# Held sums between two recurrent layers, and normalisation block by block ahead of the first sweep

## What is computed

```
x = x + L0(gn(x))    # attention over channels with a depthwise 3x3 convolution
x = x + L1(gn(x))    # four sweeps: down, up, right, left
x = x + L2(gn(x))    # the same with other weights
x = x + L3(gn(x))    # a gated MLP over tokens
gn(v): 16 groups of 3 channels; (v - mean) / sqrt(var + 1e-5) over channels and pixels
sweep: carry = row[i] + conv1d(carry, w, 5 taps) + b ; out[i] = carry
```

## Time and profile before

| what | value |
|---|---|
| median of 3 runs | 2726.66 us (2725.55 to 2729.71) |
| the profiled execution, time | 2723.77 us |
| its span, first to last instruction | 2721.6 us |
| mean granted TensorE clock | 0.95 |
| TensorE busy | 2385.1 us, 88% |
| VectorE busy | 1333.7 us, 49% |
| ScalarE busy | 770.9 us, 28% |
| GpSimd busy | 212.5 us, 8% |

### The profile page before, as it was taken

The page is one execution under the profiler, slowest core; times in us unless marked ns, Lnnn a source line. Parts: engine busy times, 40 slices in busy tenths (PEclk is TensorE's granted clock), DMA queues, the critical chain, the costliest instruction groups (busy, mean ns, idle before and its releaser), DMA issues.

```text
span 2721.6 us, 45615 instructions
## 1 busy us (share of the span) xinstructions
PE 2385.1 (88%) x18588; PEld 2127.3 (78%) x18588; DVE 1333.7 (49%) x3212; ACT 770.9 (28%) x1190; POOL 212.5 (8%) x259
## 2 busy tenths in 40 slices
PE   1999999999999799999999990599999999952785
PEld 1999948957953399999999990599999999951453
DVE  3323354344355544444555557444444555566855
ACT  3533254354356400243002551200441000002441
POOL 2000000000000180000000004500000000000311
PEclk9999999999999899999999995799999999976888
DMA  8840000004001320000000008500000000049734
GB/s 154 146 86 7 1 1 1 1 1 93 1 1 24 70 48 1 1 1 1 1 1 1 1 1 252 131 1 1 1 1 1 1 1 1 1 126 268 243 104 128
DMA packets 75558, 129.88 MB, mean 48 GB/s; under 512 B 10224, under 2 KB 59600, under 8 KB 70448
## 3 DMA queue, kind: packets, MB, share of 16 engines
q1 hardware_dynamic: 68064, 123.36, 19.0%
q10 hardware_dynamic: 7184, 3.84, 0.6%
q0 software_dynamic: 128, 0.01, 0.0%
HBM read 76.85 MB, written 50.33 MB: 47 GB/s over the span
## 4 chain that ended last, share of the span: by engine, by line
PE 80%; DVE 6%; DMA 5%; ACT 4%; issue 2%; SPq 2%; POOL 1%; ACTq 0%; POOLq 0%; DVEq 0%
PE bank L978 18%; PE bank L979 16%; PE bank L980 16%; PE bank L881 14%; PE bank L943 6%; PE bank L896 3%; PE bank L886 3%; ACT work L644 3%; DMA work<-saved 2%; PE bank L1087 2%; DMA work<-in_x 1%; DMA saved<-image 1%; SPq L335 1%; PE bank L1058 1%; DMA image<-flat_rows 1%
## 5 line engine op out<-in xcount | busy, mean ns | idle before, releaser
L1302 DVE TENSOR_TENSOR image<-bank,image 112x128 f32<-112x128 f32 x2032 | 660.4, 325 | 712.8 <-PE bank L980 712.8
L978 PE MATMUL bank<-image,scan_wt 112*112 112x128 f32 x4064 | 808.3, 280 | 36.4 <-ACT image L718 29.7
L979 PE MATMUL bank<-image,scan_wt 112*112 112x126 f32 x4064 | 770.9, 271 | 0.0
L980 PE MATMUL bank<-image,scan_wt 112*112 112x126 f32 x4064 | 769.7, 270 | 0.0
L978 PEld LDWEIGHTS bank<-image,scan_wt 112*112 112x112 f32 x4064 | 566.1, 175 | 40.6 <-ACT image L718 29.9
L979 PEld LDWEIGHTS bank<-image,scan_wt 112*112 112x112 f32 x4064 | 581.2, 176 | 0.0
L980 PEld LDWEIGHTS bank<-image,scan_wt 112*112 112x112 f32 x4064 | 578.6, 176 | 0.0
L881 PE MATMUL bank<-work 112*128 112x192 f32 x2304 | 423.9, 332 | 10.5 <-issue 10.5
L644 ACT ACTIVATE work<-image,gn_shift,gn_scale 48x567 f32<-48x567 f32 (+5 forms) x384 | 334.6, 904 | 317.0 <-PE bank L886 220.3
L881 PEld LDWEIGHTS bank<-work 112*128 112x128 f32 x2304 | 374.9, 192 | 12.9 <-issue 12.4
L736 ACT COPY work<-image 48x256 f32 x192 | 80.3, 418 | 731.7 <-PE bank L980 731.3
(11 more groups left out here) (151 smaller groups left out, 1496.6 us busy)
## 6 DMA issues: line engine op xcount, KB each, us to landing
work<-saved SPq DMA_DIRECT2D x64, 384.0 KB, 10.4
image<-flat_rows SPq DMA_DIRECT2D x4, 3072.0 KB, 18.7
out<-image SPq DMA_DIRECT2D x8, 1536.0 KB, 7.2
saved<-image SPq DMA_DIRECT2D x12, 768.0 KB, 9.9
saved<-image SPq DMA_DIRECT2D x6, 1536.0 KB, 15.6
flat_rows<-image SPq DMA_DIRECT2D x46, 192.0 KB, 6.1
band<-in_x SPq DMA_DIRECT2D x16, 384.0 KB, 5.4
work<-in_x SPq DMA_DIRECT2D x16, 384.0 KB, 5.4
```

Of the source, the lines that this page charges most:

```text
L978: mm(dst, wt[:, 1], src, start=True, stop=False)
L979: mm(dst[:, 1:J2, :], wt[:, 0], src[:, 0:J2 - 1, :], start=False, stop=False)
L980: mm(dst[:, 0:J2 - 1, :], wt[:, 2], src[:, 1:J2, :], start=False, stop=True).then_inc(s_prod[g], 1)
L1302: v.tensor_tensor(line(g, along_w, at), prod, line(g, along_w, src), ALU.add).then_inc(s_state[g], 1)
```

## The change

- The unit between the layers becomes the piece (two runs of 1024 elements of a pair) in place of the chunk. VectorE adds the even pieces, GpSimd the odd ones.
- `back` has six buffers (`GAP`): the five `kept` and one more. Six pieces are fetched ahead. While piece t < `HELD` = 10, its sum is written in place and piece t + 6 is fetched into its buffer. The sums of the last six pieces are written into their buffers, `summed(t)`, and `image` keeps layer 1's raw result there until the normalisation reads the held sum and writes `image`.
- Every piece is saved by itself as soon as it is summed; the last six are saved from the buffers.
- The normalisation of both layers is split: block 0 of pair 0 on ScalarE and block 0 of pair 1 (piece 8) on VectorE let the first sweep start. In layer 1, ScalarE then does blocks 1 to 7 of both pairs; in layer 2 it does all of pair 0 first and blocks 1 to 7 of pair 1 after the norm of pair 1. `s_ready` counts them, and TensorE and VectorE wait for it at every sixteenth row of the first sweep. `s_tail` is gone.
- The four normalisations between the stages of the last output convolution are gone.
- Before an in-place normalisation an engine waits only for the save of what it overwrites: the quarter in layer 1, the pieces of the pair below 10 in layer 2, nothing for held sums.
- GpSimd's constants and SyncE's fetches for the token stage now wait for `s_late` (the last six saves) and `s_ready`.

```diff
-VCH = 2
-V_COLS = 5120
+GAP = 6
+HELD = 2 * (K2 // 8) - GAP
-        back = kept[0:PER]
+        back = kept + [cut(at - 256 - CHUNK, [CHUNK], P)]
...
+        def piece(buf, t):
+
+            if buf is image:
+                g, n = t // NBLK, t % NBLK
+                v = image[0:P, g * 2 * IMG:(g + 1) * 2 * IMG].rearrange("p (s n) -> p s n", s=2)
+                return v[:, :, n * 2 * BN:(n + 1) * 2 * BN]
+            return buf.rearrange("p (s n) -> p s n", s=2)
+
+        def summed(t):
+
+            return piece(image if t < HELD else back[t % GAP], t).rearrange("p s (n b) -> p b s n", b=2)
+
+        def unsaved(eng, layer, t):
+
+            if layer == 0:
+                eng.wait_ge(*((s_save, 32) if t < NBLK else (s_raw[t % NBLK // 2], 32)))
+            elif t < HELD:
+                eng.wait_ge(s_keep[t // NBLK], 32 * (NBLK, HELD - NBLK)[t // NBLK])
...
-            for c in range(PER):
-                bring(c)
-            for b in range(NB - 1):
-                for m in range(PER):
-                    if m < VCH:
-                        sp.wait_ge(s_kept_v, b * VCH + m + 1)
-                    else:
-                        sp.wait_ge(s_kept_p, b * (PER - VCH) + m - VCH + 1)
-                    bring((b + 1) * PER + m)
-                save_columns(b, 0, IMG)
-            sp.wait_ge(s_kept_v, NB * VCH)
-            save_columns(NB - 1, 0, VCH * CHUNK)
-            sp.wait_ge(s_kept_p, NB * (PER - VCH))
-            save_columns(NB - 1, VCH * CHUNK, IMG)
-            sp.wait_ge(s_keep[0], 64)
-            sp.wait_ge(s_keep[1], 96)
+            for t in range(GAP):
+                bring(t)
+            for t in range(2 * NBLK):
+                sp.wait_ge((s_kept_v, s_kept_p)[t % 2], t // 2 + 1)
+                if t < HELD:
+                    bring(t + GAP)
+                save(t, s_keep[t // NBLK] if t < HELD else s_late)
+            sp.wait_ge(s_keep[0], 32 * NBLK)
+            sp.wait_ge(s_keep[1], 32 * (HELD - NBLK))
+            sp.wait_ge(s_late, 32 * GAP)
+            sp.wait_ge(s_ready, 2 * (NBLK - 1))
...
-            for m in range(KEPT):
-                nc.gpsimd.memset(kept[m][32:HALF, :], 0.0).then_inc(s_back_gap, 1)
+            for m in range(GAP):
+                nc.gpsimd.memset(back[m][32:HALF, :], 0.0).then_inc(s_back_gap, 1)
...
+            for t in range(1, 2 * NBLK, 2):
+                pool.wait_ge(s_back[t % GAP], 32 * (t // GAP + 1))
+                dst = piece(image if t < HELD else back[t % GAP], t)
+                nc.gpsimd.tensor_tensor(dst, piece(image, t), piece(back[t % GAP], t), ALU.add).then_inc(s_kept_p, 1)
+
+            pool.wait_ge(s_late, 32 * GAP)
+            pool.wait_ge(s_ready, 2 * (NBLK - 1))
...
+            def normalise(layer, t):
+
+                act.wait_ge(s_gn, 2 * layer + 3 + t // NBLK)
+                unsaved(act, layer, t)
+                src = summed(t) if layer else piece(image, t).rearrange("p s (n b) -> p b s n", b=2)
+                dst = piece(image, t).rearrange("p s (n b) -> p b s n", b=2)
+                for i in range(2):
+                    b = t // NBLK * 2 + i
+                    last = nc.scalar.activation(dst[:, i], src[:, i], ACT.Identity, bias=gn_shift[0:P, b:b + 1],
+                                                scale=gn_scale[0:P, b:b + 1])
+                return last
...
-                elif 2 <= n < 6:
-                    last = normalise(0, n // 2 - 1, n % 2 * SUB, (n % 2 + 1) * SUB)
-            last.then_inc(s_state[0], 1)
...
-                    for b in range(2):
-                        last = normalise(layer, b, 0, IMG)
-                    last.then_inc(s_state[0], 1)
+                normalise(layer, 0).then_inc(s_state[0], 1)
+                for n in range(1, NBLK if layer else 1):
+                    normalise(layer, n)
                 deviation(2 * layer + 3, 2, NB)
-                for b in (2, 3):
-                    last = normalise(layer, b, V_COLS, IMG)
-                last.then_inc(s_tail, 1)
+                for n in range(1, NBLK):
+                    if layer == 0:
+                        normalise(layer, n)
+                    normalise(layer, NBLK + n).then_inc(s_ready, 1)
...
+                if scan == 0 and at and at % 16 == 0:
+                    pe.wait_ge(s_ready, layer * (NBLK - 1) + at // 16)
...
-                pe.wait_ge(s_tail, layer + 1)
...
+                if scan == 0 and at % 16 == 0:
+                    dve.wait_ge(s_ready, layer * (NBLK - 1) + at // 16)
...
+                    for t in range(0, 2 * NBLK, 2):
+                        dve.wait_ge(s_back[t % GAP], 32 * (t // GAP + 1))
+                        dst = piece(image if t < HELD else back[t % GAP], t)
+                        v.tensor_tensor(dst, piece(image, t), piece(back[t % GAP], t), ALU.add).then_inc(s_kept_v, 1)
+                        if t % NBLK:
+                            sums(t - 1)
+                        last = sums(t)
+                        if t % NBLK == NBLK - 2:
+                            sums(t + 1).then_inc(s_stat, 2)
+                        if t == NBLK - 2:
                             dve.wait_ge(s_stat, X_STATS + NB + 2)
                             group_norm(4, P, NSTAT, 0, 2)
...
+                unsaved(dve, layer, NBLK)
                 for b in (2, 3):
-                    dve.wait_ge((s_save, s_keep)[layer][b // 2], RAW_SAVED[layer][b // 2])
-                    cols = image_n[:, b // 2, b % 2, 0:V_COLS]
+                    cols = piece(image, NBLK).rearrange("p s (n b) -> p b s n", b=2)[:, b - 2]
                     last = v.tensor_scalar(cols, cols, gn_scale[0:P, b:b + 1], gn_shift[0:P, b:b + 1],
                                            ALU.mult, ALU.add)
                 last.then_inc(s_state[1], 1)
```

72 lines of the change are left out of this document (28 added, 44 removed).

## The result

| what | before | after |
|---|---|---|
| median of 3 runs | 2726.66 us (2725.55 to 2729.71) | 2686.37 us (2685.25 to 2696.02) |
| the profiled execution, time | 2723.77 us | 2685.25 us |
| its span | 2721.6 us | 2683.4 us |
| mean granted TensorE clock | 0.950 | 0.955 |

The medians differ by 40.3 us; the ratio is 0.986, with a 95% interval of 0.9823 to 0.9897 (28 to 48 us). The changed kernel was run again later as a control: 2690.05 us against 2725.12 us, ratio 0.9871 (0.9855 to 0.9888), so 35.1 us faster. The forecast was 2692 us, 34.7 us less than before. The two profiled executions shown here differ by 38.5 us.

What follows compares the result with a forecast made beforehand. The recurrent sweeps were taken as a serial chain with TensorE busy, so mainly stages where it idles could move. Savings of 1.7 + 11.1 + 21.9 = 34.7 us gave 2692 us, range 2682 to 2706.

Steps and rivals of the forecast that it cites:

- (a): End of the last output convolution: removing four ScalarE normalisations saves 1.7 us, bounds 1.0 and 1.9.
- (b): Gap ahead of layer 1: TensorE restarts at 933.3 instead of 944.46, 11.1 us less, bounds 10.0 and 11.3.
- a clock that stays up: Restart of layer 1: if TensorE's clock did not drop, some 1.7 us more gain; not booked.
- (c): First sweeps: normalisation moved under them and the added waits cost nothing, bounds 0 and 0.7 us of loss.
- no idle time every sixteenth row: Sign expected in the sweeps: 0.65 us a half step, without idle time at the rows with added waits.
- (d): Adds between the layers: 61.3 us of VectorE work plus 9.5 us of waits, last statistic ending at 1704.2.
- (e): DMA between the layers: 290 GB/s with fetches and saves alternating, last fetch landing at 1690, in time for GpSimd's last add.
- (f): End of the gap between layers: restart at 1710.0 against 1731.87, 21.9 us less, nothing waiting for the held sums' saves.
- ScalarE late: Rival, layer 2: pair 0's normalisation on ScalarE delays the deviation, some 7 us late, 2699; chance 0.14.
- More collisions: Rival, between the layers: more VectorE adds blocked by GpSimd or late fetches, 12 to 18 us later, 2704 to 2710; chance 0.14.
- The DMA rate: Rival, between the layers: mixed traffic at one direction's pace, gains used up at 160 GB/s, 2736 at 145; chance 0.05.
- It does nothing there: Rival, end of the gap between layers: the wait for saves only moves, its 7.7 us stay, 2700; chance 0.07.

Runs made afterwards that it cites:

- d3: Changed kernel with ScalarE's four 4096-element normalisations put back between the stages of the last output convolution; 2692.85 us (1 run).
- d2: Changed kernel plus idle TensorE matmuls during the waits for the norm (4 and 5 ahead of layer 1, 14 and 5 between layers); 2695.09 us, 0.9901 of the kernel before.
- e1: Changed kernel plus fewer idle TensorE matmuls (4 and 3 ahead of layer 1, 12 and 3 between layers); 2690.27 us, 0.9876 of the kernel before.
- c3: Changed kernel with TensorE's first sweep of each layer waiting for all normalised blocks at its start; 2736.66 us, 1.0045 of the kernel before.
- e2: Changed kernel with all sixteen adds between the layers on VectorE and none on GpSimd; 2695.13 us (1 run).
- e3: Changed kernel with each GpSimd add split into two instructions of 1024 elements; 2687.12 us, 0.9862 of the kernel before.
- c4: Changed kernel with four buffers in place of six; 2690.13 us, 0.9865 of the kernel before.
- c2: Changed kernel without held sums: all sixteen written in place, pair 1's normalisation waiting for every save; 2688.07 us, 0.9876 of the kernel before.
- d4: The kernel before, unedited, profiled once more; 2726.32 us (1 run).
- d1: Changed kernel with VectorE's adds reordered to run two pieces ahead of its statistics; 2687.83 us, 0.9882 of the kernel before.

## Why the prediction was right, point by point

**(a) End of the convolution: right, a little low.** From the stage of block 2 to that of block 7, 906.33 - 861.88 = 44.4 us, against 46.4: 2.0 us less, forecast 1.7 and just above the upper bound of 1.9. The last convolution matmul ends 2.1 us earlier. d3 puts 1.9 of it on the four normalisations.

**(b) Ahead of layer 1: the instant right, two steps of the reasoning wrong.** The two short instructions took 1.54 us where I took 1.3 (bounds 1.2 and 2.3), and block 8's quarter had long been saved. Pair 1's first step came at 931.62, forecast 933.3 less the 1.7 us of (a). But 944.46, from which I counted, is the first step of pair 0. TensorE's timeline of the kernel before, then of the changed one, has both pairs' first products:

```profile
944.46 0.77 PE L978 MATMUL bank<-image,scan_wt 112*112 112x128 f32 x2 [13.89 <-ACT image L718]
...
945.87 0.63 PE L978 MATMUL bank<-image,scan_wt 112*112 112x128 f32 x2
```

```profile
928.50 0.75 PE L1003 MATMUL bank<-image,scan_wt 112*112 112x128 f32 x2
...
931.62 0.77 PE L1003 MATMUL bank<-image,scan_wt 112*112 112x128 f32 x2 [1.54 <-DVE image L1357]
```

Before, TensorE waited for all normalising (`s_tail`) and then did both pairs. With the change it does pair 0's step while VectorE is still at the norm of pair 1, which the prediction did not count. So pair 1's first step came 14.25 us earlier and not 12.8. Layer 1's end came only 11.76 us earlier. Two things took the 2.5 us back. The larger is TensorE's clock, which I had booked at no change. Windows of TensorE at the start of the sweep, of the changed kernel and then of the kernel before (the granted clock is the number before the last two):

```profile
931.60:937.70 6.10, 6.08 (x29) 6.08 (x30) 1.33 (x5) 6.10 (x6) 5.98 (x4) 0.50 0.26 54
```

```profile
944.50:948.60 4.10, 4.10 (x20) 4.10 (x21) 0.58 (x2) 0.00 (x0) 4.10 (x3) 0.53 0.00 0
```

A half step costs 1.27 instead of 0.65 us there. VectorE's second add of the sweep, the first of pair 1, came 14.11 us earlier than before, its eighth, when both kernels are at 0.65 us, only 12.46 us earlier: 1.65 us for the clock. In d2 and e1, where TensorE did not pause, the stretch vanished and 1.6 to 2.3 us came back. The case of a clock that stays up, priced at 1.7 us in the prediction, is therefore a true mechanism with about the right price; the change alone does not get it. The other part, 0.85 us, belongs to (c). That the two errors of (b) and the one of (c) left layer 1's end within 1.1 us of the forecast is luck.

**(c) The moved normalisation: the cover right, the zero wrong.** ScalarE's instructions took 1.22 us rather than 1.13 and the cover was still about fourfold, so no step waited for a block. c3 shows what stands behind that: 46.6 us, if the sweep had to wait for them. But the added waits are not free. VectorE's timeline at the first of the sixteenth rows, with the change:

```profile
954.37 0.29 DVE L1328 TENSOR_TENSOR image<-bank,image 112x128 f32<-112x128 f32 x1 [0.43 <-PE bank L1005]
954.95 0.29 DVE L1328 TENSOR_TENSOR image<-bank,image 112x128 f32<-112x128 f32 x1 [0.29 <-PE bank L1005]
955.72 0.29 DVE L1328 TENSOR_TENSOR image<-bank,image 112x128 f32<-112x128 f32 x1 [0.48 <-PE bank L1005]
```

Three half steps take 2.06 us instead of the 1.94 that they take elsewhere, and so at each of the seven rows. From the ninth to the 241st add of the first sweep it takes 150.4 us in both layers of both profiles of the kernel before, and 151.3 us in both layers of the change and of the control: 0.85 us a layer, 1.7 us in all. In c3, where TensorE has lost its seven waits and VectorE has kept its own, it takes 150.8 us, so each engine's waits make about half. ScalarE is not the cause: it has long finished when the last of these rows are reached, and they lose the same. The prediction put this term at nothing because VectorE's wait of 0.36 us for a product would swallow it, with 0.7 us as its bound; it lies above the bound, and one of its own signs, no idle time every sixteenth row, did not come true.

**(d) The adds: the sum right, its parts only roughly.** The statistics ended 69.4 us after the first add, forecast 70.8. The waits that I had written out by hand were 2.0 and 4.1 us for pieces 2 and 4 and 1.2, 0.3 and 1.9 us for later ones, 9.5 us together. Measured were 1.8 and 4.0 us for pieces 2 and 4, 1.9 us for piece 10, and 1.3 us on the norm of pair 0, 9.0 us together. The first two are fixed, since GpSimd works without a pause from 1621.8 to 1645.8. The later ones hang on when fetches land: in the control they made 4.2 us more, and in d2's profile the stretch was 8.7 us longer. So the forecast lies inside a scatter that it did not name, and that the profile after agrees to 1.4 us is partly luck. VectorE's own work was a little overcounted too: 9.58 us for 16 statistics is 38.3 us for 64, not 38.6. The possibility that the two-element instructions of the norm could wait was missing in the prediction, and they gave the largest single wait in the control (4.18 us). The rule of the Trainium skill that the prediction weighed (SBUF — State Buffer, SBUF: two separate sides) speaks of VectorE operations with two SBUF inputs. The trace agrees for these as well: 4.34 us instead of 0.16 behind a GpSimd add that had started 0.17 us before. e2 confirms the cause; e3, where halves of GpSimd's add made the waits half as long, the size.

**(e) DMA: right.** I took 290 GB/s. Busy time in two long windows of the changed kernel's gap:

```profile
1625.00:1665.00 40.00, 1.06 (x4) 0.90 (x4) 38.17 (x49) 1.52 (x3) 34.69 (x7) 0.50 0.94 316
1665.00:1692.00 27.00, 0.00 (x0) 0.00 (x0) 26.96 (x35) 18.03 (x16) 8.09 (x2) 0.50 0.98 285
```

The last fetch landed at 1676.3 (GpSimd's last add starts then, after a wait of 8.35 us for it), which is 54.6 us after the first add, forecast 56.6. Taken together the two windows are 303 GB/s, a little above what I took. c4 shows that the number of buffers, which I named as what takes the waits away, does not decide.

**(f) The end of the gap: the time right, the reason wrong.** From the last statistic to pair 1's first step it took 6.0 us, forecast 5.8 (4.4 + 1.3 + 0.1, here 4.42 + 1.54 + 0.06). But the sentence "the six last sums are kept in the buffers and read from there, so nothing waits for their saves" gave the credit to the held sums, and c2 shows that without them nothing waits either. What the profiles offer instead is this. Before, the last statistics followed GpSimd's last add at once, and the save that the normalisation waited for was two chunks, asked for only after that add. With the change each piece is saved when it is summed, the last add on VectorE ends at 1683.97, and 7.2 us of statistics and 4.4 us of norm lie behind it. c2 has this order too, with everything in place, so the held sums are not needed for it. That I did not run the order and the size of the saves apart from each other, or from the rest of the change, leaves open which of them does it.

**The sum.** By the instants that the prediction used, the profile's parts are 11.8 us up to the end of layer 1, and 98.45 - 75.46 = 23.0 us between the layers: 34.75 us, forecast 34.7. Layer 2 repeats what (b) and (c) showed. Pair 1's first step came 36.1 us earlier than before (1733.26 and 1697.12), the longer low clock took back 0.7 us and the waits of (c) 0.85, and layer 2 ends 34.4 us earlier. The agreement to 0.4 us is luck in part: the steps of pair 0 done under the norms (some 1.4 us in each layer) were not in the sum, nor were the clock and the waits, which took away 4.0 us together, and the collisions came out 1.4 us lower. And it holds for this profile alone. In the control's, layer 2 ends 29.8 us earlier than in the first profile before and 33.1 us earlier than in d4.

The spans of the two profiles differ by 38.2 us. The remaining 3.8 us of these came from the last 300 us of the kernel, which the change does not touch in what it computes. There the kernel before gave 305.4 and 304.7 us, the change 301.6 and 301.2 us, and no profile with the change in it reached 304.7. I had no such term. Most of it is there early in the stage, at the add that waits for the last fetch of `saved[1]`. VectorE's timeline, before and after:

```profile
2504.09 2.36 DVE L1353 TENSOR_TENSOR image<-image,work 112x1024 f32<-112x1024 f32 x2 [1.98 <-DMA work<-saved]
```

```profile
2465.99 2.36 DVE L1379 TENSOR_TENSOR image<-image,work 112x1024 f32<-112x1024 f32 x2 [1.79 <-DMA work<-saved]
```

Counted from the stage's first add, at 2416.21 and 2381.82, that is 87.88 and 84.17 us, 3.7 of the 3.8. In d4 it is 88.63 and in the control 86.35 us, 2.3 us of 3.4. Further on VectorE waits for TensorE's products, but that wait is 12.41 us before and 12.40 after, at a granted clock of 0.71 in the 17.4 us ahead of this instruction in both (in d1 it is 8.71 us, at 0.90), so it does not part these two profiles. Why those fetches, or the adds that they feed, are through sooner with the change stays open. Without this stage the medians' 35.1 and 40.3 us would, by these profiles, lie 3 to 4 us lower, so the forecast's number for the whole kernel was helped by a term that it did not have.

**The rivals.** *ScalarE late* fell: 11.3 us idle ahead of the deviation, 9.7 us in the control, forecast 7. *More collisions* came in part: +4.2 us in the control's profile and +8.7 in d2's, of the 12 to 18 that it was priced at. *The DMA rate* fell, with 316 and 285 GB/s in mixed traffic. *It does nothing there* fell in its time (no wait for a save), and the held sums themselves did nothing, for the other reason: there was no such wait left for them to take away.

## What to carry over

Where an in-place step waits for a save, try saving in small pieces as they become ready and giving the first consumer a small first block; extra buffers to keep results out of the way are worth a trial without them, since here they gained nothing that could be measured. Price the waits that such a release adds to a serial chain, also when they are met: here 0.12 us each time both engines had one. When VectorE and GpSimd share work on operands in SBUF, count as exposed every two-input instruction of VectorE, the tiny ones of a serial chain too, and expect a scatter of up to one or two GpSimd instructions (8.7 us here). Work that fills a wait on the bounding engine must end just as the wait does, so start it from an event whose distance to the end of the wait is fixed, and measure that distance before choosing the count. Compare the same instant before and after: the first step of a stage can be another one in the changed kernel.

## What the runs showed of the hardware that was not expected

- A VectorE instruction on 112x2 elements with two SBUF inputs took 4.34 us behind a GpSimd add of 4.50 us, 0.16 us otherwise, and 2.24 us behind half an add.
- The DMA queues moved 316 GB/s over 40 us of alternating fetches and saves of 384 KB, where fetches alone were at 170.
- In d2 TensorE's granted clock was 1.00 over a pause of 3.1 us and 0.52 in the 2.9 us of small products behind it. With the change the low level lasted for 6.1 us from pair 1's first step, which stood behind a pause of 1.5 us; before, it lasted for 4.1 us from pair 0's.
- A wait that had long been met, one on TensorE and one on VectorE at a row of the sweep, lengthened the chain by 0.12 us, and by 0.06 us where only VectorE had one (c3).
